# The first variance with rows on the free axis, its root on ScalarE and GpSimd, and the second scores moved forward

## The reference

```
z = (h - mean(h)) / sqrt(var(h) + eps)
h = h + softmax(q k^T / 8) v Wo^T + bo
w = softmax over the two largest of (xn Wr + br)
h = h + sum over e of w[e] * (gelu(xn W1[e] + b1[e]) W2[e] + b2[e])
```

## Time and profile before

| | us |
|---|---|
| median of 3 runs | 264.24 |
| lowest, highest | 263.4, 267.89 |
| the profiled execution | 259.98 |
| its span in the profile | 257.8 |

### The profile page before, as it was taken

The page is one execution under the profiler, slowest core; times in us unless marked ns, Lnnn a source line. Parts: engine busy times, 40 slices in busy tenths (PEclk is TensorE's granted clock), DMA queues, the critical chain, the costliest instruction groups (busy, mean ns, idle before and its releaser), DMA issues.

```text
span 257.8 us, 5026 instructions
## 1 busy us (share of the span) xinstructions
PE 225.0 (87%) x1585; PEld 126.3 (49%) x1585; DVE 168.5 (65%) x512; ACT 139.7 (54%) x341; POOL 119.1 (46%) x112
## 2 busy tenths in 40 slices
PE   0579986979797999998989899999999999999991
PEld 0436764646465666676654254445344443443430
DVE  4996787887969787576574457284665638274353
ACT  1311384565656575747585536554566556457640
POOL 2515250434525252243123558458565636656652
PEclk9999999999999999999999999999999999999998
DMA  4156331223322320212444580672749376293911
GB/s 112 35 142 187 85 115 42 100 92 99 84 86 67 116 71 32 69 32 72 118 115 100 133 193 3 143 153 62 169 87 232 82 176 166 54 231 91 208 32 32
DMA packets 19795, 27.20 MB, mean 106 GB/s; under 512 B 5306, under 2 KB 16826, under 8 KB 19770
## 3 DMA queue, kind: packets, MB, share of 16 engines
q10 hardware_dynamic: 6256, 13.50, 22.3%
q1 hardware_dynamic: 13514, 13.38, 19.5%
HBM read 24.89 MB, written 1.98 MB: 104 GB/s over the span
## 4 chain that ended last, share of the span: by engine, by line
PE 55%; DVE 14%; issue 10%; DMA 9%; POOL 4%; SPq 3%; ACT 3%; DVEq 0%; POOLq 0%; ACTq 0%
PE PD L943 18%; PE PD L957 16%; DVE ahead L1127 4%; DMA rdbc<-rdend 3%; PE PD L869 3%; SPq L305 2%; PE PD L893 2%; DVE nmax L1171 2%; POOL rstd L447 2%; PE PD L903 2%; DMA srow<-scored 2%; PE PD L919 2%; ACT E L596 2%; PE PD L847 2%; PE PD L858 2%
## 5 line engine op out<-in xcount | busy, mean ns | idle before, releaser
L1280 DVE SCALAR_TENSOR_TENSOR ye<-PD,b_col,mb 128x408 f32<-128x408 f32 x64 | 40.8, 640 | 47.3 <-PE PD L957 46.5
L635 ACT ACTIVATE hid<-PD,b_eff 128x816 f32<-128x816 f32 x64 | 56.6, 935 | 27.3 <-PE PD L943 23.3
L471 POOL TENSOR_TENSOR acc<-acc,ye 128x408 f32<-128x408 f32 x52 | 54.7, 1052 | 32.2 <-DVE ye L1280 29.7
L943 PE MATMUL PD<-uT,w_g 64*128 64x408 f32 x256 | 53.1, 530 | 0.4 <-ACT hid L635 0.4
L957 PE MATMUL PD<-hid,w_sb 128*64 128x408 f32 x256 | 51.2, 519 | 0.2 <-DVE ye L1280 0.2
L596 ACT ACTIVATE E<-PD,nmax 102x204 f32<-102x204 f32 x64 | 26.5, 422 | 21.1 <-DVE nmax L1171 21.1
L943 PEld LDWEIGHTS PD<-uT,w_g 64*128 64x128 f32 x256 | 21.9, 186 | 19.2 <-ACT hid L635 6.1
L957 PEld LDWEIGHTS PD<-hid,w_sb 128*64 128x64 f32 x256 | 15.5, 136 | 32.0 <-issue 26.9
L447 POOL TENSOR_TENSOR rstd<-veps,neg_half 102x8 f32<-102x8 f32 x8 | 13.1, 1638 | 35.3 <-DVE veps L1144 35.3
L453 POOL TENSOR_TENSOR rstd<-veps,neg_half 102x8 f32<-102x8 f32 x8 | 13.1, 1639 | 29.8 <-DVE veps L1198 29.8
L1127 DVE SCALAR_TENSOR_TENSOR ahead<-srow,score,PD 128x256 bf16<-128x256 f32 x56 | 23.4, 474 | 1.8 <-DMA srow<-scored 1.8
(11 more groups left out here) (153 smaller groups left out, 332.4 us busy)
## 6 DMA issues: line engine op xcount, KB each, us to landing
mb<-mixd ACTq DMA_DIRECT2D x28, 408.0 KB, 5.7
srow<-scored SPq DMA_DIRECT2D x7, 512.0 KB, 3.9
rdbc<-rdend SPq DMA_DIRECT2D x16, 102.0 KB, 2.9
rbc<-rstd2d SPq DMA_DIRECT2D x16, 102.0 KB, 2.8
mb<-mixd SPq DMA_DIRECT2D x4, 408.0 KB, 5.2
X<-in_x ACTq DMA_DIRECT2D x6, 256.0 KB, 3.0
rbc<-rstdd SPq DMA_DIRECT2D x14, 102.0 KB, 2.8
out<-y SPq DMA_DIRECT2D x7, 204.0 KB
```

What stands on the lines that cost most here:

```text
L471: pool.tensor_tensor(acc[n % 4][:, :], H[:, n, :] if e == 0 else acc[n % 4][:, :], ye[k % 4][:, :], ALU.add)\
L635: act.activation(hid[k % 4][:, :, :], hid_ps[k % 2][:, :, 0:C], ACT.Gelu, bias=b1_eff[:, e:e + 1]).then_inc(hid_ok, 1)
L943: last = pe.matmul(hid_ps[k % 2][:, p, 0:C], w1_g[halves[p], e, :], uT[halves[p], n, :], start=True, stop=True)
L1280: dve.scalar_tensor_tensor(out=ye[k % 4][:, :], in0=y_ps[k % 2], scalar=b2_col[:, e:e + 1], in1=mb[n % MB][:, e, :], op0=ALU.add, op1=ALU. ...
```

## The change

- `variance` takes a 128x32 matrix of ones (columns 0 and 1 hold the halves, the rest is 0) as weights and lets the squares move, 102 columns each. The variances come out as 4 x 32 partitions x 102; partitions 32g and 32g + 1 hold group g of the two halves.
- The root is taken from that form: ScalarE computes ln(var + eps), var + eps, and exp(-0.5 ln) as `root`; GpSimd makes one Newton step, r (1.5 - 0.5 v r r), with four operations that each wait for the one before. `var_eps`, `turn_std` and the copy of the transpose are gone.
- `write_std` writes two pieces (partitions p, p+32, ... of rstd), and `read_std` waits for both.
- One table set with logarithm and exponential is loaded at the start on ScalarE. The router's gap of unit 0 is made with an exponential, and three more operations of VectorE turn that into the tanh.
- On PE `variance` stands before `values`, and `scores(u, 1)` before `attend(u, 1)`.
- On ScalarE `copy_denT`, `copy_OT`, `gap_tanh` and `exp_neg` stand behind the exponentials; `squares2` stands between the halves of the second softmax.
- On VectorE `one_over_den` stands behind `normalise` and compare 1, and `row_max` 1 directly behind `row_max` 0, ahead of `normalise2` and `one_hot`.

```diff
             def write_std(u):
-                sp.wait_ge(rstdT_ok, u)
-                sp.dma_start(rstdd[u], rstdT[:, :]).then_inc(rstdd_ok, 16)
+                sp.wait_ge(rstd_ok, u + 1)
+                for p in range(2):
+                    sp.dma_start(rstdd[u, p * G:(p + 1) * G, :], rstd[p:P:32, :]).then_inc(rstdd_ok, 16)
...
             def inverse_std(u):
                 pool.wait_ge(veps_ok, u + 1)
-                if u >= 1:
-                    pool.wait_ge(rstdTp_ok, u)
-                pool.tensor_tensor(rstd[:, :], veps[:, :], neg_half[:, :], ALU.pow).then_inc(rstd_ok, 1)
+                pool.wait_ge(root_ok, u + 1)
+                pool.tensor_tensor(mend_a[:, :], veps[:, :], root[:, :], ALU.mult).then_inc(mend_ok, 1)
+                pool.wait_ge(mend_ok, 3 * u + 1)
+                pool.tensor_tensor(mend_b[:, :], mend_a[:, :], root[:, :], ALU.mult).then_inc(mend_ok, 1)
+                pool.wait_ge(mend_ok, 3 * u + 2)
+                pool.tensor_scalar(mend_a[:, :], mend_b[:, :], -0.5, 1.5, ALU.mult, ALU.add).then_inc(mend_ok, 1)
+                pool.wait_ge(mend_ok, 3 * u + 3)
...
+                pool.tensor_tensor(rstd[:, :], mend_a[:, :], root[:, :], ALU.mult).then_inc(rstd_ok, 1)
...
+            def root_std(u):
+                act.wait_ge(varp_ok, u + 1)
+                if u >= 1:
+                    act.wait_ge(rstd_ok, u)
+                act.activation(log_v[:, :], var_ps, ACT.Ln, bias=eps_col[:, 0:1]).then_inc(log_ok, 1)
+                act.activation(veps[:, :], var_ps, ACT.Identity, bias=eps_col[:, 0:1]).then_inc(veps_ok, 1)
+                act.wait_ge(log_ok, u + 1)
+                act.activation(root[:, :], log_v[:, :], ACT.Exp, scale=-0.5).then_inc(root_ok, 1)
...
+            act.add_instruction(mybir.InstLoadActFuncSet(name=nc.get_next_instruction_name(),
+                                                         engine=mybir.EngineType.Activation, act_func_set_id=LN_EXP))
...
                     copy_k(u)
-                    softmax(u, 0, [0])
-                if s >= 1:
-                    copy_stdT(s)
+                root_std(s)
                 if (u := unit(s, 1)) is not None:
-                    softmax(u, 0, [1])
+                    softmax(u, 0)
+                    softmax(u, 1, [0])
+                if (u := unit(s, 3)) is not None:
+                    squares2(u)
+                if (u := unit(s, 1)) is not None:
+                    softmax(u, 1, [1])
                 if (u := unit(s, 2)) is not None:
                     copy_denT(u)
-                if (u := unit(s, 3)) is not None:
-                    squares2(u)
+                    copy_OT(u)
                 if s == UNITS - 1:
                     gap_tanh(0)
...
-            def turn_std(u):
-                pe.wait_ge(rstd_ok, u + 1)
-                pe.transpose(rstdT_ps, rstd[:, :], ident[0:Q, 0:Q]).then_inc(rstdTp_ok, 1)
-
...
-                    last = pe.matmul(var_ps.rearrange("q (p g) -> q p g", g=G)[:, :, g], sq[:, g * Q:(g + 1) * Q], ones2[:, :],
+                    last = pe.matmul(var_ps[32 * g:32 * (g + 1), :], ones32[:, :], sq[:, g * Q:(g + 1) * Q],
...
+                variance(s)
+                if (u := unit(s, 1)) is not None:
                     values(u)
-                variance(s)
...
-                if s >= 1:
-                    turn_std(s)
+                if (u := unit(s, 1)) is not None:
+                    scores(u, 1)
...
+                    if n == 0:
+                        dve.tensor_scalar(one_over[:, :], tanh[:, :], 1.0, None, ALU.add).then_inc(lean_ok, 1)
+                        dve.wait_ge(lean_ok, 1)
+                        dve.reciprocal(share[:, :], one_over[:, :]).then_inc(lean_ok, 1)
+                        dve.wait_ge(lean_ok, 2)
+                        dve.tensor_scalar(tanh[:, :], share[:, :], 2.0, -1.0, ALU.mult, ALU.add).then_inc(lean_ok, 1)
...
-                if (u := unit(s, 2)) is not None:
-                    one_over_den(u)
                 normalise(s - 1)
                 if (u := unit(s, -1)) is not None:
                     compare(u, 1)
+                if (u := unit(s, 2)) is not None:
+                    one_over_den(u)
...
                 row_max(s - 1, 0)
+                row_max(s - 1, 1)
...
-                row_max(s - 1, 1)
```

More of the change, by code:

```diff
@@ L80, in audio_tower_kernel @@
         ones2 = sb("ones2", [P, 2])
+        ones32 = sb("ones32", [P, 32])
         tie = sb("tie", [P, 3, P])
@@ L130, in audio_tower_kernel @@
         sq = sb("sq", [P, C])
-        veps = sb("veps", [Q, 2 * G])
-        rstd = sb("rstd", [Q, 2 * G])
-        rstdT = sb("rstdT", [2 * G, Q])
+        veps = sb("veps", [P, Q])
+        log_v = sb("log_v", [P, Q])
+        root = sb("root", [P, Q])
+        mend_a = sb("mend_a", [P, Q])
+        mend_b = sb("mend_b", [P, Q])
+        rstd = sb("rstd", [P, Q])
+        eps_col = sb("eps_col", [P, 1])
         rbc = sb("rbc", [P, C])
@@ L165, in audio_tower_kernel @@
         tanh = sb("tanh", [Q, 2 * G])
+        one_over = sb("one_over", [Q, 2 * G])
+        share = sb("share", [Q, 2 * G])
         lean = sb("lean", [Q, 2 * G, NE])
@@ L237, in audio_tower_kernel @@
         mb_in = [[sem(f"mb_in{i}_{h}") for h in range(2)] for i in range(MB)]
+        lean_ok = sem("lean_ok")
         TOP = 17
@@ L248, in audio_tower_kernel @@
         K = UNITS * NE
+        LN_EXP = 6
         def unit(s, lag):
@@ L444, in inverse_std @@
                 pool.wait_ge(veps_ok, u + 1)
-                if u >= 1:
-                    pool.wait_ge(rstdTp_ok, u)
-                pool.tensor_tensor(rstd[:, :], veps[:, :], neg_half[:, :], ALU.pow).then_inc(rstd_ok, 1)
+                pool.wait_ge(root_ok, u + 1)
[5 more added lines that the diff above has]
+                pool.wait_ge(mend_ok, 3 * u + 3)
+                if u == 1:
+                    pool.wait_ge(spread0_ok, 1)
+                if u >= 2:
+                    pool.wait_ge(rstdd_ok, 32 * (u - 1))
+                pool.tensor_tensor(rstd[:, :], mend_a[:, :], root[:, :], ALU.mult).then_inc(rstd_ok, 1)
             def inverse_std2(u):
@@ L621, in gap_tanh @@
                 act.wait_ge(top, TOP * n + 13)
-                act.activation(tanh[:, :], gap[:, :], ACT.Tanh, scale=0.5).then_inc(tanh_ok, 1)
+                if n == 0:
+                    act.activation(tanh[:, :], gap[:, :], ACT.Exp, scale=-1.0).then_inc(tanh_ok, 1)
+                else:
+                    act.activation(tanh[:, :], gap[:, :], ACT.Tanh, scale=0.5).then_inc(tanh_ok, 1)
             def copy_mT(n):
@@ L696, in _ @@
                     exp_neg(u)
-                if (u := unit(s, 1)) is not None:
-                    softmax(u, 1)
             copy_mT(0)
@@ L814, in variance @@
                 for g in range(G):
-                    last = pe.matmul(var_ps.rearrange("q (p g) -> q p g", g=G)[:, :, g], sq[:, g * Q:(g + 1) * Q], ones2[:, :],
+                    last = pe.matmul(var_ps[32 * g:32 * (g + 1), :], ones32[:, :], sq[:, g * Q:(g + 1) * Q],
                                      start=True, stop=True)
                 last.then_inc(varp_ok, 1)
-            def turn_std(u):
-                pe.wait_ge(rstd_ok, u + 1)
-                pe.transpose(rstdT_ps, rstd[:, :], ident[0:Q, 0:Q]).then_inc(rstdTp_ok, 1)
             def spread_std0():
                 pe.wait_ge(rstd_ok, 1)
-                for p in range(2):
-                    for g in range(G):
+                for g in range(G):
+                    for p in range(2):
                         last = pe.matmul(rstd0_ps[halves[p], g * Q:(g + 1) * Q],
-                                         rstd[:, p * G + g:p * G + g + 1].to_broadcast([Q, D]), ident[0:Q, 0:Q],
-                                         start=True, stop=True)
-                last.then_inc(rstdTp_ok, 1)
+                                         ident[:, 32 * g + p:32 * g + p + 1].to_broadcast([P, D]),
+                                         rstd[:, :], start=True, stop=True)
+                last.then_inc(spread0_ok, 1)
             def turn_den(u):
@@ L1008, in _ @@
                     centre2(u)
-                if (u := unit(s, 1)) is not None:
-                    scores(u, 1)
                 if (u := unit(s, 3)) is not None:
@@ L1075, in _ @@
             dve.memset(tie[:, :, :], -2e-38)
+            dve.memset(eps_col[:, :], EPS)
             dve.memset(ident[:, :], 0.0).then_inc(dve_prep, 1)
@@ L1078, in _ @@
             dve.memset(ones2[:, :], 0.0)
+            dve.memset(ones32[:, :], 0.0)
             dve.memset(wq_bd[:, :], 0.0)
@@ L1138, in one_hot @@
                     .then_inc(pick_ok, len(prs))
-            def var_eps(u):
-                dve.wait_ge(varp_ok, u + 1)
-                if u >= 1:
-                    dve.wait_ge(rstd_ok, u)
-                dve.tensor_scalar(veps[:, :], var_ps, EPS, None, ALU.add).then_inc(veps_ok, 1)
             def normalise(u):
@@ L1287, in _ @@
```

(2 more changed lines are left out.)

20 lines of the change are left out of this document (8 added, 12 removed).

## The result

| | before | after |
|---|---|---|
| median of the runs shown, us | 263.82 (4) | 272.69 (4) |
| lowest, highest | 261.05, 267.89 | 269.61, 274.98 |
| the profiled execution, its span | 259.98, 257.8 | 271.97, 270.2 |

The ratio is 1.033 (95%: 1.018 to 1.049): slower, 3 us above the forecast of 269.7. That is inside the stated range of 263 to 274, but outside the forecast's own 268 to 272. The profiled executions lie 12.0 apart; I forecast 5.5.

A forecast was written before the change was run, and what follows sets the result against it. The prediction saw a ring of waits closed by VectorE in passes 3 to 5, the rbc reads setting the pass after the change. Passes 1 to 6 +3.9, pass 7 +1.6: +5.5 on 264.24 gives 269.7 us, range 263 to 274.

The forecast's parts named there:

- The queue behind `copy_denT`: ScalarE's new order puts copy_denT at +10.5 instead of +7.7, rbc at +14.5; z waits, passes 4 to 6 take 14.5 us.
- z(6) to project(7): Pass 7, judged by the last project: the router's steps and later rbc add 1.6 us (0 to 2.5) to 14.93.
- The landing: The second rbc read lands 2.8 us after its issue, so rbc arrives 4.0 us after copy_denT.
- Pass 1: Second scores' maxima stand behind the expert biases on PE and ahead of pick on VectorE: 0.4 us more (-0.5 to +1).
- From the profile to the median: The runs' median, 264.24, lies 4.3 us above the profiled execution, 259.98; the 5.5 was added to that median.
- Looser ring: Rival: squares2 not late or variance matmuls overlap fully; copy_denT near +9.7, passes 4 to 6 13.7 us; 266.7 us, chance 0.25.
- VectorE stays the bound: Rival: reads land by about +12, VectorE's idle time falls from 2.33 to about 1.0 us; 259.7 us, chance 0.1.
- Tighter tail: Rival: later rdbc holds residual(5), second-norm reads wait; 1 us in pass 7, 0.5 in six more; 273.7 us, chance 0.16.
- Tables thrash: Rival: ScalarE loads tables at each function change, 1.3 us more in each of eight steps; 280 us, chance 0.04.
- The small prices: Root operations on ScalarE 0.3 us each, Newton operations on POOL 0.35 each, variance matmuls on PE 0.6.

The follow-up runs named there:

- experiment 1: The changed kernel with read_std(s) moved ahead of write_den(s-2) on SP: 268.6 us, ratio 1.027 (1.016 to 1.038).
- experiment 2: The changed kernel with copy_denT and copy_OT behind softmax(0), ahead of the second softmax, on ScalarE: 265.5 us, ratio 1.015 (1.002 to 1.028).
- experiment 5: The kernel before with only ScalarE's order changed to the new one: 287.3 us, no interval; 1.08 by the medians.
- experiment 10: The changed kernel with copy_denT and copy_OT ahead of the second softmax, plus unread filler matmuls on PE: 267.1 us, ratio 1.022 (1.010 to 1.034).
- experiment 11: The changed kernel with copy_denT and copy_OT ahead of the second softmax, normalise2 between the row maxima and unread filler matmuls on PE: 266.1 us, no interval.
- experiment 3: The changed kernel with normalise2 between the two row maxima on VectorE: 269.6 us, no interval.

## Why the prediction was right, and where not

*The queue behind `copy_denT`*, the forecast's main step, held to a tenth or two in pass 5: v at +4.04 (forecast 4.32), second maxima +6.63 (6.73), `centre2` +8.34 (8.4), `squares2` +9.30 (9.3), `copy_denT` +10.52 (10.5), `var_eps2` +10.8 (10.7), rstd for SP at +6.3 (6.5). Experiments 1 and 2 removed the wait of z, each from another side, but for one of 0.56 and one of 0.74; experiment 5 brought it up alone.

*Term by term, z to z:*

| pass | forecast | measured | the difference |
|---|---|---|---|
| 1 | 14.1 | 16.82 | +2.7 |
| 2, 3 | 13.05, 13.75 | 12.92, 13.43 | -0.4 |
| 4 | 14.5 | 15.08 | +0.6, the read's landing |
| 5 | 14.5 | 15.43 | +0.9, the read's landing |
| 6 | 14.5 | 16.16 | +0.3 landing, +1.4 the clock |
| z(6) to project(7) | 16.53 | 16.98 | +0.4 |

Together +5.9; behind project(7) 1.0 more (135.74 against 134.70, the first 4.5 us at half clock). With the forecast 5.5 that is 12.4, the difference of the spans.

*The landing* was mis-sized: 2.8 by the median of its issues, but 3.38, 3.73 and 3.10 for the second read in passes 4 to 6. Why these three are slower isn't settled.

*Pass 1* was the worst term: +0.4 taken (to +1), +3.1 measured against the earlier trace rows. PE's rows in it, its busy time over `centre`, and VectorE's copy of v:
```profile
27.54 1.83 PE L791 MATMUL PD<-beta_col,w_raw 64*128 64x1 f32 x8 [1.60 <-DMA w_raw<-in_L_ffn_W]
29.30 1.73 PE L838 MATMUL PD<-H,center 128*128 128x408 f32 x2
...
29.00:31.00 2.00, 2.00 (x5) 0.92 (x5) 0.87 (x6) 0.00 (x0) 0.00 (x0) 1.00 0.04 9
...
34.57 0.77 DVE L1181 TENSOR_TENSOR v<-PD,vbias 102x264 f32<-102x264 f32 x2 [4.70 <-PE PD L882]
```
The same copy in the kernel before, and the copy and the whole pass in experiment 10, whose program is that of the changed kernel up to the end of pass 1:
```profile
31.37 0.77 DVE L1162 TENSOR_TENSOR v<-PD,vbias 102x264 f32<-102x264 f32 x2 [1.48 <-PE PD L858]
...
30.79 0.77 DVE L1191 TENSOR_TENSOR v<-PD,vbias 102x264 f32<-102x264 f32 x2 [1.91 <-PE PD L884]
...
26.65:40.68 14.03, 12.00 (x106) 8.79 (x107) 10.94 (x34) 8.49 (x28) 4.79 (x8) 0.88 0.30 88
```
PE now waits for the experts' weights ahead of `centre`, and `centre` and the projections take 1.7 to 1.9 times as long as in the kernel before, so v comes at +6.93 in place of +3.73. Behind v nothing is lost: z(1) follows it by 9.89 us, and by 9.98 in the kernel before, although `pick` now stands behind the second maxima. In experiments 10 and 11 the same order has v at +4.14 and +4.07 and passes of 14.03 and 13.97. So the term that I named was right, and what failed is one that the sum didn't have: the wait of 1.60 for the weights and the slow PE behind it. It isn't in every execution, and what decides it isn't known.

*The clock* wasn't in the forecast at all. These are three stretches of the changed kernel (between them it is 1.00; a fourth lies in pass 1), then two groups of PE, one at each level, and last one of the kernel before:
```profile
81.00:85.00 4.00, 4.00 (x29) 3.19 (x30) 2.86 (x13) 1.89 (x7) 2.65 (x2) 0.57 0.19 58
...
101.00:106.00 5.00, 3.95 (x30) 1.91 (x31) 3.19 (x13) 1.13 (x3) 1.04 (x1) 0.66 0.28 65
...
129.00:139.00 10.00, 9.03 (x57) 7.04 (x57) 5.39 (x19) 2.81 (x7) 2.68 (x2) 0.51 0.36 93
...
86.62 0.92 PE L838 MATMUL PD<-H,center 128*128 128x408 f32 x2 [0.29 <-DVE zT L1173]
...
102.05 1.70 PE L838 MATMUL PD<-H,center 128*128 128x408 f32 x2 [2.26 <-DVE zT L1173]
...
42.08 0.93 PE L810 MATMUL PD<-H,center 128*128 128x408 f32 x2 [2.19 <-DVE zT L1154]
```
At 102.05 PE had stood idle for 2.26 us, waiting for z behind the late read; the same `centre` took 1.70 instead of 0.92, and row maxima and `copy_denT` of pass 6 all came 1.4 later. So in this pass the queue is paid twice, once as a wait and once as a slower engine behind it. The Trainium skill, "TensorE: Matmul & The Clock Gate", section on why this matters for kernels, says that PE should have no long pauses between bursts, since an idle stretch brings the clock back to half. The trace agrees only in part. At 102.05 the fall (0.50 is 1.2 GHz) does lie behind a pause. At 81 it came while PE was busy, behind pauses of only 0.73 and 0.60 us, and the kernel before paused for 2.19 ahead of 42.08 and kept 1.00. So the rows don't say what exactly starts a fall.

*From the profile to the median.* I added 4.3 us, the distance of the profiled execution of before from its median, as if it were a constant. It isn't: before's profiled execution had a clock of 0.995, and 34 others of that kernel lie between 258.97 at 0.997 and 269.4 at 0.953. After's has 0.960 and lies 0.7 under its median. By the profiles I was 6.5 short; the 4.3 made up for much of it, though it has nothing to do with pass 1, the landings and the clock that the sum lacked. That the number came within 3 us was partly luck.

*The rivals.* Looser ring: no, `copy_denT` stood at +10.5. VectorE stays the bound: not here, but experiment 2 fulfils its condition (`write_den` at +7.9 in pass 4), and the passes gave 2.2 of the 4.5 promised; what failed in it is the idle time, 1.0 taken and 2.24 measured, since the wait ahead of `var_eps2` wasn't in it and the one before v didn't shrink as far. Tighter tail: its 273.7 is nearer to the 272.7 measured than my 269.7, but not by its mechanism. z(7) did wait (1.40), but for `rbc`; between z(0) and z(7) `residual` waited once for GpSimd's scaling, which `rdbc` had held, 1.14 us in pass 3, and not in pass 7. Tables thrash: no. The profile has two loads again, as in the earlier trace rows:
```profile
L682 ACT ACT_TABLE_LOAD x1 | 1.3, 1283 | 4.5 <-issue 4.5
L739 ACT ACT_TABLE_LOAD x1 | 1.3, 1283 | 0.0
...
L579 ACT ACTIVATE root<-log_v 128x102 f32<-128x102 f32 x8 | 2.4, 302 | 0.0
```
The trace thus agrees with the Trainium skill, "ScalarE: Activation LUTs", section on table sets, which has logarithm and exponential in one set: the logarithm (L576) and this exponential alternate eight times between the two loads. The small prices were close: root 0.3 each (0.30 to 0.35), Newton 0.35 (0.28 to 0.41), variance 0.6 (0.38: its four groups overlap nearly as far as my lower bound).

*What stays open:* why the reads land late in passes 4 to 6; what starts each fall of the clock; the share of the weights' DMA in pass 1, and why PE is slow behind it; how much the late `variance2` costs by itself; the totals of experiments 3 and 11.

## What to carry to other kernels

Before an instruction is moved later on one engine, follow what it feeds into every in-order queue: here a copy of 0.23 us, 2.8 us later, held a DMA queue in which an unrelated result, long ready, stood behind it. Time won at one wait of a bounding engine counts only if its next waits are priced too. Moving work on one engine also moves what a second engine does last before the next pass: `variance2`, late by over a microsecond, was hidden as long as the queue was worse. And a wait that ends in a pause of TensorE can cost twice; look at the granted clock of several executions before taking one profile's distance to the median as a constant.

## What the runs showed of the hardware that was not expected

- TensorE's granted clock falls to 0.50 for stretches of 3.5 to 10 us, and where they fall differs between executions and kernels. Time follows it roughly: on one chip the kernel before took 258.97 us at 0.997 and 268.1 at 0.965, but also 264.3 at 0.983 and 264.1 at 0.964. One execution of experiment 1's kernel had a mean of 0.586 and took 374 us, beside 267.0 at 0.947.
- Matmuls whose result nobody reads can make a kernel faster (0.989, 0.982 to 0.996, for the kernel before), where they lie in PE's pauses; where they delay `values`, they don't (9.2 us of waits in place of 3.4). That the clock is the reason isn't shown for every kernel: in the changed one it hardly rose.
- A granted clock of 1.00 in the record doesn't always mean full speed: `centre` at 29.30 took 1.73 us and at 86.62 took 0.92, both at a recorded 1.00.
